# The correction's two products on separate halves of the TensorE array, with each chunk's corrected bits copied four times

## The reference

```python
xn = _layernorm(x)
# branch 1: a circular filter over the 256 numbers, 24 latent bits, a Golay correction, a projection back
x1 = real(ifft(fft(xn) * filt))                      # filt depends on a global fractal dimension
bits = (x1 @ W_el + b_el) > 0                        # 24 bits a token
corrected = _golay_correct(bits)
branch1 = x1 + corrected @ W_le + b_le               # 24 -> 256
# branch 2: a feed-forward layer
branch2 = gelu(xn @ w1 + b1) @ w2 + b2               # 256 -> 1024 -> 256
out = x + branch1 + branch2
```

## Time and profile before

| | before |
|---|---|
| median of 3 runs | 408.56 us |
| the profiled execution's own time | 408.33 us |
| its span, first to last instruction | 406.5 us |
| TensorE (PE) busy | 401.1 us, 99% of the span |
| VectorE (DVE) busy | 298.1 us, 73% |
| ScalarE (ACT) busy | 223.3 us, 55% |
| GpSimd (POOL) busy | 88.2 us, 22% |
| mean granted TensorE clock | 0.999 |

### The profile page before, as it was taken

One profiled execution on the slowest core, in us unless ns is written; L12 is line 12 of the kernel. 1 busy time (PEld: TensorE's weight loads), 2 busy tenths in 40 slices (PEclk: granted clock), 3 DMA queues, 4 the chain that ended last, 5 costly groups with the idle time before them and its releaser, 6 DMA issues.

```text
span 406.5 us, 5533 instructions
## 1 busy us (share of the span) xinstructions
PE 401.1 (99%) x1768; PEld 328.7 (81%) x1768; DVE 298.1 (73%) x511; ACT 223.3 (55%) x333; POOL 88.2 (22%) x102
## 2 busy tenths in 40 slices
PE   8999999999999999999999999999999999999996
PEld 4888888888888888888888888888888888888885
DVE  6889975878668795677957688486874879657654
ACT  3966646457354764537545464555636556364551
POOL 3153411313003131121313013131121313013000
PEclk9999999999999999999999999999999999999999
DMA  7544333213333213232123333023333121111011
GB/s 203 200 157 156 103 105 104 67 40 102 105 104 103 58 46 104 103 103 104 53 54 100 103 104 102 29 75 103 104 103 102 49 56 52 52 52 52 2 52 52
DMA packets 15307, 35.75 MB, mean 88 GB/s; under 512 B 5440, under 2 KB 6592, under 8 KB 15296
## 3 DMA queue, kind: packets, MB, share of 16 engines
q1 hardware_dynamic: 15152, 35.49, 26.5%
q10 hardware_dynamic: 144, 0.13, 0.1%
HBM read 27.17 MB, written 8.45 MB: 88 GB/s over the span
## 4 chain that ended last, share of the span: by engine, by line
PE 97%; DVE 1%; DMA 1%; POOL 0%; SPq 0%; issue 0%; DVEq 0%
PE p_h L955 43%; PE p_f L973 28%; PE p_f L978 14%; PE p_s L1012 5%; PE p_l L999 4%; PE p_s L1020 2%; DMA x_sb<-x 1%; DVE xt_sb L790 0%; SPq L246 0%; DVE stats L821 0%; POOL row_nums L359 0%; DVE rows_sb L808 0%; PE p_f L988 0%; DVE xT_lo L830 0%; DVE w_lo L795 0%
## 5 line engine op out<-in xcount | busy, mean ns | idle before, releaser
L444 ACT ACTIVATE h<-p_h,small_sb 128x512 f32<-128x512 f32 x128 | 88.2, 689 | 141.6 <-PE p_h L955 141.3
L631 DVE TENSOR_TENSOR h_lo<-h,h_hi 128x512 fp32r<-128x512 f32 x128 | 103.0, 804 | 71.2 <-ACT h_hi L452 71.2
L973 PE MATMUL p_f<-h_hi,w_hi 128*128 128x512 f32 x254 | 99.3, 391 | 0.0
L973 PE MATMUL p_f<-h_hi,w_lo 128*128 128x512 f32 x254 | 98.9, 389 | 0.0
L367 POOL TENSOR_TENSOR uv<-xn 128x512 f32<-128x512 f32 x30 | 59.3, 1998 | 125.9 <-DVE xn L616 125.9
L452 ACT CAST h_hi<-h 128x512 fp32r<-128x512 f32 x128 | 79.5, 621 | 5.8
L955 PE MATMUL p_h<-xT_hi,w_hi 128*128 128x512 f32 (+1 forms) x258 | 79.4, 389 | 0.0
L955 PE MATMUL p_h<-xT_lo,w_hi 128*128 128x512 f32 (+1 forms) x258 | 79.2, 388 | 0.1
L955 PE MATMUL p_h<-xT_hi,w_lo 128*128 128x512 f32 (+1 forms) x258 | 79.3, 389 | 0.0
L978 PE MATMUL p_f<-h_lo,w_hi 128*128 128x512 f32 x254 | 78.2, 389 | 0.0
L955 PEld LDWEIGHTS p_h<-xT_lo,w_hi 128*128 128x128 f32 x258 | 48.3, 188 | 10.6 <-DVE xT_lo L830 0.3
(11 more groups left out here) (112 smaller groups left out, 319.8 us busy)
## 6 DMA issues: line engine op xcount, KB each, us to landing
xt_sb<-xt SPq DMA_DIRECT2D x16, 512.0 KB, 5.3
x_sb<-x SPq DMA_DIRECT2D x15, 512.0 KB, 4.7
rows_sb<-rows_dram SPq DMA_DIRECT2D x15, 512.0 KB, 4.3
out<-xt_sb SPq DMA_DIRECT2D x15, 512.0 KB, 2.9
xt_sb<-w SPq DMA_DIRECT2D x3, 512.0 KB, 7.2
xt_sb<-w SPq DMA_DIRECT2D x2, 256.0 KB, 4.2
x_sb<-x SPq DMA_DIRECT2D x2, 128.0 KB, 2.1
x_sb<-x SPq DMA_DIRECT2D x1, 256.0 KB, 3.0
```

The costliest lines, as they stand in the source:

```text
L444: nc.scalar.activation(h[m % 2][:], p_h[:, m % 2, :], ACT.Gelu, bias=small_sb[:, S_B1 + m:S_B1 + m + 1]).then_inc(gelu_done, 1)
L631: nc.vector.tensor_tensor(h_lo[m % HR][:], h[m % 2][:], h_hi[m % HR][:].bitcast(F32), ALU.subtract).then_inc(h_lo_done, 1)
L973: mm(p_f[:, a, :], w[:, m, a * HF:(a + 1) * HF], h_hi[r][:], start=(m == 0 and w is w2_hi), stop=False, skip_group_check=True)
```

## The change

The corrected bits of the two chunks of a pair go to two tiles, `cor[0]` and `cor[1]`. Each holds four copies of its chunk's 32 rows, made by four casts of 32 rows in two calls of `corrected`. The weights become one tile `le2` of 128 columns: rows 0 to 63 hold high and low part for the sums, rows 64 to 127 those for the differences. `le_products` makes the sums' product from rows 0 to 63 and the differences' from rows 64 to 127, each a matmul of 64 rows. The calls move: `le_products(0, p)` from after block 4 to after block 5, in the last chunk `le_products(1, p)` from block 6 to block 7; VectorE's `add_sums` in odd chunks and in the last chunk comes behind `hidden_lo(c, 5)`. The copies for the pair's second chunk are made in the even chunk that follows. The tiles that TensorE reads (`c_hi`, `c_lo`, `cw`, `le2`, `cor`) are declared earlier. Two memsets of `le2` on GpSimd go.

```diff
+        c_hi = sb("c_hi", [P, 2, HF], F32R)
+        c_lo = sb("c_lo", [P, 2, HF], F32R)
+        cw = [sb(f"cw{i}", [P, KB, P], F32R) for i in range(2)]
+        le2 = sb("le2", [P, HF], F32R)
+        cor = [sb(f"cor{i}", [P, CTOK], F32R) for i in range(2)]
         small_sb = sb("small_sb", [P, S_END], F32)
...
-        cor = sb("cor", [P, CTOK], F32R)
-        le2 = [sb(f"le2_{i}", [P, 2, HF], F32R) for i in range(2)]
...
-                nc.gpsimd.memset(le2[q][:].bitcast(F32), 0.0).then_inc(le_set, 1)
...
-            def corrected(p, first=False):
+            def corrected(p, q, a, freed):
                 act.wait_ge(turned_back, p + 1)
-                if not first:
-                    act.wait_ge(le_done, 2 * p)
-                for at in (0, PAIR):
-                    nc.scalar.copy(cor[at:at + PAIR, :], word_out[:]).then_inc(cor_done, 1)
+                if freed is not None:
+                    act.wait_ge(le_done, freed)
+                for at in (PAIR * a, PAIR * a + SEG):
+                    nc.scalar.copy(cor[q][at:at + SEG, :], word_out[SEG * q:SEG * q + SEG, :]).then_inc(cor_done, 1)
...
@@ ScalarE: even_chunk @@
+                    if m == 0:
+                        corrected(p, 1, 0, 2 * p + 1)
                     if m == 1:
                         turned_hi(c)
+                    if m == 2:
+                        corrected(p, 1, 1, 2 * p + 1)
@@ ScalarE: odd_chunk @@
                     if m == 3:
-                        corrected(p)
+                        corrected(p, 0, 0, 2 * p - 1)
                     if m == 4:
+                        corrected(p, 0, 1, 2 * p - 1)
                         columns_hi(c + 1, 0)
@@ ScalarE: last_chunk @@
-                    if m == 3:
-                        corrected(p)
+                    if m in (3, 4):
+                        corrected(p, 0, m - 3, 2 * p - 1)
+                    if m in (5, 6):
+                        corrected(p, 1, m - 5, 2 * p)
@@ VectorE: odd_chunk @@
                 hidden_lo(c, 4)
-                add_sums(b)
                 columns_lo(c + 1, 0)
                 hidden_lo(c, 5)
+                add_sums(b)
+                hidden_lo(c, 6)
                 add_differences(b)
-                hidden_lo(c, 6)
@@ VectorE: last_chunk @@
                 hidden_lo(c, 4)
+                hidden_lo(c, 5)
                 add_sums(b)
                 add_differences(b)
-                hidden_lo(c, 5)
                 hidden_lo(c, 6)
@@ TensorE @@
             def le_products(par, p):
-                pe.wait_ge(cor_done, 2 * (p + 1))
+                pe.wait_ge(cor_done, 8 * p + 4 * (par + 1))
                 for a in range(2):
-                    last = mm(p_s[:, a, :], le2[par][:, a, :], cor[:], start=False, stop=True, skip_group_check=True)
+                    at = slice(PAIR * a, PAIR * a + PAIR)
+                    last = mm(p_s[:, a, :], le2[at, :], cor[par][at, :], start=False, stop=True, skip_group_check=True)
                 last.then_inc(le_done, 1)
@@ TensorE: odd_chunk @@
-                    if m == 4:
+                    if m == 5:
                         le_products(0, p)
@@ TensorE: last_chunk @@
-                    if m == 4:
+                    if m == 5:
                         le_products(0, p)
                     if m == 6:
                         filtered(c)
+                    if m == 7:
                         le_products(1, p)
```

More of the change, by code:

```diff
@@ L111, in build @@
         c_f = sb("c_f", [P, 2, HF], F32)
-        c_hi = sb("c_hi", [P, 2, HF], F32R)
-        c_lo = sb("c_lo", [P, 2, HF], F32R)
-        cw = [sb(f"cw{i}", [P, KB, P], F32R) for i in range(2)]
         stats = sb("stats", [P, CT, 6], F32)
@@ L176, in build @@
         latent_in, stored = sem("latent_in"), sem("stored")
-        idle_set, pool_set, cw_set, le_set = sem("idle_set"), sem("pool_set"), sem("cw_set"), sem("le_set")
+        idle_set, pool_set, cw_set = sem("idle_set"), sem("pool_set"), sem("cw_set")
         w1_hi_ready, w1_ready = sem("w1_hi_ready"), sem("w1_ready")
@@ L452, in hidden_hi, with even_chunk @@
                 nc.scalar.copy(h_hi[m % HR][:], h[m % 2][:]).then_inc(h_hi_done, 1)
-            def even_chunk(c):
+            def even_chunk(c, p):
                 for m in range(MB):
@@ L483, in first_branch_chunk @@
                         turned_hi(c)
+                    if m == 3:
+                        corrected(p, 0, 0, None)
                     if m == 4:
                         columns_hi(c + 1, 0)
-                        corrected(p, first=True)
+                        corrected(p, 0, 1, None)
             def last_chunk(c, p):
@@ L561, in _ @@
             act.wait_ge(le_first, 1)
[L562 to L565, removed]
+            for a in range(2):
+                at = slice(PAIR * a, PAIR * a + SEG)
+                nc.scalar.copy(le2[at, :], le_h[at, a, :].bitcast(F32)).then_inc(le_copied, 1)
             first_branch_chunk(1, 0)
             with act.Fori(1, CHUNKS // 2 - 1) as i:
-                even_chunk(2 * i)
+                even_chunk(2 * i, i - 1)
                 odd_chunk(2 * i + 1, i)
-            even_chunk(CHUNKS - 2)
+            even_chunk(CHUNKS - 2, CHUNKS // 2 - 2)
             last_chunk(CHUNKS - 1, CHUNKS // 2 - 1)
@@ L665, in turn_back @@
                 if not first:
-                    dve.wait_ge(cor_done, 2 * p)
+                    dve.wait_ge(cor_done, 8 * p)
                 nc.vector.transpose(word_out[:], by_token[:, :, :].rearrange("p b l -> p (b l)")).then_inc(turned_back, 1)
@@ L910, in _ @@
             dve.wait_ge(le_first, 1)
[L911 to L915, removed]
+            for a in range(2):
+                at = slice(PAIR * a + SEG, PAIR * a + PAIR)
+                nc.vector.scalar_tensor_tensor(out=le2[at, :], in0=le_t[at, a, :], scalar=0.5,
+                                               in1=le_h[at, a, :].bitcast(F32), op0=ALU.mult,
                                                op1=ALU.subtract).then_inc(le_ready, 1)
```

## The result

The changed kernel takes 412.35 us (median of 6 runs, 412.07 to 413.34), the kernel before 408.63 (6 runs, 408.33 to 408.80). The ratio is 1.0094 with a 95% interval of 1.0084 to 1.0104: slower by 0.9%, where 0.5% faster was forecast, and 0.85 us above the range.

What follows compares the result with a forecast made beforehand. TensorE, busy 99% of the span, was taken as the bound. 3.2 us saved in 14 calls less 1.2 lost in the last chunk gave -2.0, from 408.56 to 406.6 us; range 405.4 to 411.5.

Steps and rivals of the forecast that it cites:

- The bound: Whole kernel: TensorE is busy 99% of the span, without a gap from 59 to 379 us; only the ends differ.
- the full overlap: Calls in chunks 1 to 14: two products side by side cost one matmul, saving 0.227 us each, 3.2 in all.
- either case that I priced: Second half's weight load: hidden under the matmul ahead, or 0.11 us late, saving 0.12 a call (408.2 us, chance 0.17).
- ScalarE's copies: Casts in both chunks of a pair: 3.7 us more work, covered; rival of late copies gives 409, chance 0.04.
- 1.2 us was forecast for its order: Last chunk: waits for VectorE's differences and `hidden_lo(15, 7)` make the kernel end 1.2 us later.
- 1.4 for products that don't overlap: Last chunk's loss in the no-overlap rival, where 32 matmuls stay at 0.227 us: 410.0 us, chance 0.13.
- TensorE's two waits: Last chunk: `filtered(15)` stands 0.6 us for VectorE's differences; `last_down`, possible at 401.62, starts at 402.6 after `hidden_lo(15, 7)`.
- second sign of a drain: At a call: the first product starts later than 0.227 us behind its predecessor, which would show the forecast wrong.
- first sign: At a call: over 0.46 us between the first product and the matmul after it, which would show the forecast wrong.
- a rival at 0.28 in all: At each call: array drains between 128 and 64 rows, up to 0.16 us twice; chance 0.22 about 411.4, 0.06 beyond 413.
- a further case "beyond 413": At each call: drain with loads exposed too, 0.11 us each, two a call, 3 us more, 414.5; chance 0.06.
- a possible -0.7: Moving `cor` and `le2` forward in SBUF might save 0.05 us a call, 0.7 in 14 calls; 0 was taken.

## Why the prediction was wrong

**What held.** The bound: between the start-up and the last chunk TensorE has no gap other than at the calls. The overlap: "the full overlap" with 0.227 a call is what the two products on one half lost (0.22). The second half's load is no obstacle; it is made beside the first, not behind it, which is better than either case that I priced. ScalarE's copies are covered, in all 14 chunks: no wait for `cor` and 343.9 us with them in. The last chunk: 1.2 us was forecast for its order, with 1.4 for products that don't overlap; measured 1.55 in the kernel before and 1.5 in the changed one, of which the old order gives back 1.2. `hidden_lo(15, 7)` decides there, as worked out. TensorE's two waits were shorter in the changed kernel, 0.19 instead of 0.6 for `filtered` and 0.69 instead of 1.0 for `last_down`, since the mode changes ahead of them had used up a part. The prediction's second sign of a drain came as well, a first product later than 0.227 behind its predecessor: it is 0.31 (220.48 - 220.17). Its first sign, over 0.46 from the first product to the matmul behind the pair, did not (0.43), since the overlap hides it.

**What failed.** The step "I take the full overlap" counted a call as the one matmul that is left, 0.23, and so the change of the mode as nothing; the sum had no term for it. It costs 0.40 a call, 0.43 with the matmuls behind it, against the overlap's 0.227. The working shows the slip: the rule cited there, that a change of the tiling mode drains the array, was read and put down as a rival at 0.28 in all, on the ground that the trace showed no such pause, though the trace had only one mode and could not show one.

**The rival was priced too low.** It had 0.16 a change, the tail of the record, and no load (411.4 us). The runs have 0.09 for the drain and 0.11 for the load, 0.20. That load was left as a further case "beyond 413", with 0.06. The two come together in every call: the load of the new mode starts only with its own matmul, 0.31 behind the last matmul of the old mode, so that the cover of every other load, the matmul ahead, is gone. The drain was priced 0.07 too high and the load, at nothing, 0.11 too low. With 0.20 the sum is 14 x (0.40 - 0.227) = 2.4, plus the 1.5 measured at the end: 408.56 + 3.9 = 412.5, before what the addresses and the matmuls behind a call change, and 412.35 was measured.

**The addresses.** I took 0 of a possible -0.7 because a mode change might disturb the stream as well. In kernels without mode changes the whole 0.7 to 0.8 is there (407.76 against 408.58). In the changed kernel the matmuls behind a call are uneven again, by 0.03 a call, so that of the 0.05 only 0.02 was saved; that is why its 14 chunks cost 2.2 and not 2.4. The guess that a mode change disturbs the stream fits this: with 128 rows and nearly the same places (a second weight tile shifts `cor` by 512 bytes) the starts are even, at 24.48 a chunk.

What is left open is why the place of tiles in SBUF changes the pace of TensorE's matmuls, and what makes the 0.03.

## What to carry to other kernels

Splitting the array pays by the matmuls that are issued between two changes of its tiling, not by the call: here a change costs 0.20 us and an overlapped matmul of 512 columns saves 0.227, so one pair between two changes loses 0.17, or 0.20 with the matmuls behind it. An estimate from these numbers is that two overlapped pairs would do little more than break even (0.45 saved for 0.40 to 0.43) and that it takes three for a clear gain; no run here had more than one. When a trace cannot show a price because the kernel never does the thing, "no such pause is seen" is no evidence against it. And an order that is free in the steady state has to be followed through the last pass, where one wait behind another turned a small change of order into 1.5 us.

## What the runs showed of the hardware

- Two products of 64 rows on different halves, fp32r, run side by side, and so do their weight loads: 0.50 us for two records of 0.498, 0.19 for two loads. The Trainium skill ("TensorE: Matmul & The Clock Gate", Part 3) gives about 4 ns between the starts of matmuls on different row groups; this trace agrees within its hundredths of a microsecond.
- A change from 128 rows to 64 or back pauses TensorE for 0.09 us and exposes a load of 0.11; two products in the same 64 rows have no pause between them. The Trainium skill's rule that changing the mode and not just the tile drains the engine ("TensorEngine Tiling (Array Packing)", Tiling Modes) holds here, with this price.
- The products' two tiles, moved forward by 12 and 18 KB in each partition together with three others that TensorE reads, made a chunk of the loop 24.48 us instead of 24.53, though most of the matmuls that got faster read other tiles. Other places of the two gave 24.50 and 24.51.
